# Flamingo gated block: keys and x batches 1 to 3 from host-transposed inputs, row statistics spread on chip, last keys among the first queries

## The reference

```
xn = layernorm(x);  fn = rmsnorm(ctx, fn_w)
Q = rmsnorm(xn @ Wq.T + bq, qn_w);  K = rmsnorm(fn @ Wk.T + bk, kn_w)
x = x + tanh(g_xattn) * softmax(Q K.T / sqrt(1024)) @ fn
zn = layernorm(x)
gate = softmax(zn @ W_gate.T); thr = sigmoid(zn @ W_thr + b_thr) / 8
w = max(gate - thr, 0), normalized over the 8 experts
x = x + tanh(g_ffn) * (zn @ W_base.T + b_base + 2 * sum_e w_e * (zn @ A_e.T) @ B_e.T)
```

## Time and profile before

| what | value |
|---|---|
| median of 3 runs | 527.96 us (527.92 to 528.04) |
| profiled execution | 526.89 us, span 525.1 us |
| PE busy | 500.9 us (95%) |
| DVE busy | 271.2 us (52%) |
| ACT, POOL busy | 153.0 and 153.4 us (29% each) |
| DMA, mean over the span | 83 GB/s |
| mean granted TensorE clock | 0.993 |

### The profile page before, as it was taken

One profiled execution on the slowest core, in us unless ns is written; L12 is line 12 of the kernel. 1 busy time (PEld: TensorE's weight loads), 2 busy tenths in 40 slices (PEclk: granted clock), 3 DMA queues, 4 the chain that ended last, 5 costly groups with the idle time before them and its releaser, 6 DMA issues.

```text
span 525.1 us, 7062 instructions
## 1 busy us (share of the span) xinstructions
PE 500.9 (95%) x2768; PEld 459.6 (88%) x2768; DVE 271.2 (52%) x584; ACT 153.0 (29%) x323; POOL 153.4 (29%) x123
## 2 busy tenths in 40 slices
PE   2589999999999999999988999999999999999997
PEld 2589888888888888888888999999999999999997
DVE  3887543525352532156568766456554565654423
ACT  4476444243223322354541112211112111111100
POOL 3456566312222221145273320122201222012200
PEclk9799999999999999999999999999999999999999
DMA  8643611111112001321550322113221112210012
GB/s 316 256 157 114 240 41 41 41 41 40 41 40 81 1 1 64 139 71 51 201 161 32 90 80 81 41 40 122 80 81 52 41 69 81 82 41 38 3 41 81
DMA packets 11617, 43.51 MB, mean 83 GB/s; under 512 B 1600, under 2 KB 1984, under 8 KB 11200
## 3 DMA queue, kind: packets, MB, share of 16 engines
q1 hardware_dynamic: 11584, 43.06, 22.6%
HBM read 34.67 MB, written 8.39 MB: 82 GB/s over the span
## 4 chain that ended last, share of the span: by engine, by line
PE 81%; DVE 10%; DMA 3%; POOL 2%; ACT 2%; issue 2%; SPq 0%; POOLq 0%; DVEq 0%; ACTq 0%
PE bank L399 11%; PE bank L401 11%; PE bank L400 11%; PE bank L467 10%; PE bank L468 10%; PE bank L466 10%; PE bank L332 6%; DMA bb<-b_base_dram 2%; PE bank L480 2%; DVE xn L710 2%; DVE small L697 1%; PE bank L482 1%; PE bank L481 1%; PE bank L417 1%; PE bank L416 1%
## 5 line engine op out<-in xcount | busy, mean ns | idle before, releaser
L466 PE MATMUL bank<-wch,zth 128*128 128x388 f32 x384 | 132.5, 345 | 0.0
L467 PE MATMUL bank<-wcl,zth 128*128 128x388 f32 x384 | 130.5, 340 | 0.0
L468 PE MATMUL bank<-wch,ztl 128*128 128x388 f32 x384 | 129.8, 338 | 0.0
L399 PE MATMUL bank<-xth,wqh 128*128 128x512 f32 x256 | 102.1, 399 | 0.0
L401 PE MATMUL bank<-xth,wql 128*128 128x512 f32 x256 | 100.0, 390 | 0.0
L400 PE MATMUL bank<-xtl,wqh 128*128 128x512 f32 x256 | 99.8, 390 | 0.0
L899 POOL TENSOR_TENSOR small<-small,mhalf 128x1 f32<-128x1 f32 (+1 forms) x42 | 25.8, 615 | 218.8 <-DVE small L702 190.2
L773 DVE SCALAR_TENSOR_TENSOR qtl<-bank,vecs,qth 128x512 fp32r<-128x512 f32 x32 | 24.0, 750 | 100.5 <-ACT sq L630 100.5
L466 PEld LDWEIGHTS bank<-wch,zth 128*128 128x128 f32 x384 | 72.2, 188 | 1.0
L467 PEld LDWEIGHTS bank<-wcl,zth 128*128 128x128 f32 x384 | 72.3, 188 | 0.6
L468 PEld LDWEIGHTS bank<-wch,ztl 128*128 128x128 f32 x384 | 72.1, 188 | 0.0
(11 more groups left out here) (113 smaller groups left out, 642.3 us busy)
## 6 DMA issues: line engine op xcount, KB each, us to landing
x<-x_dram SPq DMA_DIRECT2D x32, 512.0 KB, 3.3
out_dram<-x SPq DMA_DIRECT2D x15, 512.0 KB, 2.6
wc_raw<-wc_dram SPq DMA_DIRECT2D x3, 1552.0 KB, 6.1
wk_raw<-wk_dram SPq DMA_DIRECT2D x8, 512.0 KB, 10.6
wq_raw<-wq_dram SPq DMA_DIRECT2D x8, 512.0 KB, 5.5
fn_raw<-ctx_dram SPq DMA_DIRECT2D x8, 256.0 KB, 5.0
ctx_raw<-ctx_dram SPq DMA_DIRECT2D x2, 512.0 KB, 3.7
fnw<-fn_w_dram SPq DMA_DIRECT2D x1, 512.0 KB, 6.4
```

Of the source, the lines that this page charges most:

```text
L399: pe.matmul(acc[:, :], wqh[f][:, k, :], xth[b % 2][:, k, :], start=k == 0, stop=False)
L466: pe.matmul(acc, zth[z][:, k, :], wch[c][:, k, :], start=k == 0, stop=False)
L467: pe.matmul(acc, zth[z][:, k, :], wcl[c][:, k, :], start=False, stop=False)
L468: done = pe.matmul(acc, ztl[z][:, k, :], wch[c][:, k, :], start=False, stop=k == KB - 1)
```

## The change

The host now also passes two arrays: `xt`, x transposed by batch to [4, 128, 8, 512], and `ctxt`, the context transposed to [128, 8, 256].

Keys: `ct` multiplies the transposed raw context by fn_w per partition while splitting it (columns of `vecs`). The RMS root of each context row is applied after the key matmul: `rsb` transposes two columns of roots with a stride of zero, so that they lie along the free axis, and `k_out` multiplies by them. Key blocks 5 to 7 stand behind the queries 0 to 2.

Queries of batches 1 to 3: the raw transposed x is loaded; mean and root of each row are taken from a row-wise copy of x (`x_stat`), spread with two groups of stride-zero transposes (`mr`), subtracted on GpSimd (`zc`), multiplied on VectorE (`z`), and split (`z` on ScalarE, `zl` on VectorE). Batch 0 goes as before, from four buffers of its own (`xfirst`).

The diff, cut to the stage order, PE, SP and the new operations:

```diff
+        first = [("ct", 0), ("wk", 0), ("ct", 1), ("ct", 2), ("ct", 3), ("small",), ("wk", 1), ("k", 0), ("wk", 2),
+                 ("ctx_norm",), ("k", 1), ("wk", 3), ("ln_stat", 0), ("k", 2), ("rsb",), ("k_out", 0), ("ln_stat", 1),
+                 ("ln", 0), ("k_out", 1), ("wk", 4), ("ln", 1), ("k", 3), ("k_out", 2), ("xt", 0, 0), ("xt", 0, 1),
+                 ("ln_stat", 2), ("xt", 1, 0), ("xt", 1, 1), ("k", 4), ("ln_stat", 3), ("ln", 2), ("k_out", 3),
+                 ("wq", 0), ("xt", 2, 0), ("xt", 2, 1), ("ln", 3), ("k_out", 4), ("xt", 3, 0), ("xt", 3, 1), ("wk", 5),
+                 ("wq", 1)]
         for b in range(B):
             for f in range(FB):
+                if b + 1 < B and f < 2:
+                    first += [("x_stat", (b + 1) * TPB + 2 * f + j) for j in range(2)]
                 first.append(("q", b, f))
+                if b == 0 and f < 3:
+                    first += [("k", f + 5), ("k_out", f + 5)]
+                if b == 0 and f < 2:
+                    first.append(("wk", f + 6))
                 if b == 0 and f + 2 < FB:
                     first.append(("wq", f + 2))
+                if b == 0 and f == 2:
+                    first.append(("tanh",))
+                if b == 0 and f == 4:
+                    first.append(("k_norm",))
                 if f > 0:
                     first.append(("s", b, f - 1))
                 elif b > 0:
...
                 if b + 1 < B:
-                    first += [("xt", (b + 1) * TPB + u // NH, u % NH) for u in XT_AT[f]]
+                    if f == 2:
+                        first += [("mr", b + 1), ("zc", b + 1, 0)]
+                    if f >= 4:
+                        first.append(("zl", b + 1, f - 4))
+                    if 3 <= f < 7:
+                        first.append(("z", b + 1, f - 3))
+                    if 3 <= f < 6:
+                        first.append(("zc", b + 1, f - 2))
...
+        WK_DVE, WK_POOL = (2, 3), (1, 4, 5, 6, 7)
...
         def tensor(pe):
+                if stage == "rsb":
+                    acc = ring_open((stage,), "act")
+                    pe.wait_ge(g_const, CONSTS)
+                    pe.wait_ge(g_ctx, 1)
+                    transposes(acc, ctx_rs.unsqueeze(2).to_broadcast([P, 2, P]))
+                elif stage == "mr":
+                    b, = i
+                    pe.wait_ge(g_mr, b)
+                    for k in range(2):
+                        acc = ring_open((stage, b, k), "act")
+                        transposes(acc, ms[b % 2][:, k, :].unsqueeze(2).to_broadcast([P, TPB, P]))
...
                 elif stage == "q":
...
                     for k in range(KB):
+                        if b > 0 and f == 0 and k % CK == 0:
+                            pe.wait_ge(v_zl, 4 * (b - 1) + k // CK + 1)
...
         def sync(sp):
+            sp.dma_start(vecs[:, :, :], vec).then_inc(ld_vec, 16)
+            load_ct(0)
+            sp.dma_start(wk_raw[0][:, 0:4, :], wk[0][:, 0:4, :]).then_inc(ld_wk[0], 16)
+            sp.dma_start(wk_raw[0][:, 4:8, :], wk[0][:, 4:8, :]).then_inc(ld_wk0, 16)
+            load_ct(1)
+            load_ct(2)
+            load_ct(3)
+            load_wk(1)
+            load_wk(2)
+            load_ctx(0)
+            load_ctx(1)
+            load_wk(3)
+            load_x(0)
+            load_x(1)
+            load_wk(4)
+            load_x(2)
+            load_x(3)
+            load_wq(0)
+            load_wk(5)
+            load_wq(1)
+            load_wk(6)
+            load_wk(7)
+            load_x(TPB)
+            load_x(TPB + 1)
+            sp.dma_start(sc[:, 0:3], scal.to_broadcast([P, 3])).then_inc(ld_sc, 16)
+            sp.wait_ge(v_xn, 2)
+            load_wq(2)
+            sp.wait_ge(v_xn, 4)
+            load_wq(3)
+            sp.wait_ge(p_k, 2)
+            load_xt(1)
...
+                elif stage == "q" and 0 < i[0] < B - 1 and i[1] == 0:
+                    b, f = i
+                    sp.wait_ge(p_q, nq(b, 0))
+                    load_xt(b + 1)
                 elif stage == "load_fn":
                     b, = i
+                    if b == 0:
+                        sp.wait_ge(v_z, 4 * (B - 1))
+                        sp.dma_start(fnw[:, :], fn_w.to_broadcast([P, D])).then_inc(ld_fnw, 16)
...
         def scalar(act):
+                if stage == "ct":
+                    for k in range(CK * c, CK * c + CK):
+                        act.activation(cth[:, k, :], ct_raw[:, k, :], ACT.Copy, scale=fw[:, k:k + 1]).then_inc(a_cth, 1)
+                elif stage == "z":
+                    b, c = i
+                    kc = slice(CK * c, CK * c + CK)
+                    act.wait_ge(v_z, 4 * (b - 1) + c + 1)
...
+                    act.activation(xth[b % 2][:, kc, :], xt_raw[b % 2][:, kc, :], ACT.Copy).then_inc(a_zh, 1)
+                elif stage == "k_out":
+                    f, = i
+                    act.wait_ge(v_kr, f + 1)
+                    if f >= 2:
+                        act.wait_ge(g_ksum, max(1, f - 2))
+                    act.activation(ksq[f % 2][:, :], kr[f % 2][:, :], ACT.Square, bias=bk[:, f:f + 1]).then_inc(a_ksq, 1)
+                    act.wait_ge(v_kfull, f + 1)
...
                     act.activation(kt[:, f, :, 0:S], kfull[:, :].rearrange("p (b s) -> p b s", b=B),
                                    ACT.Copy).then_inc(a_kth, 1)
...
         def vector(dve):
+                elif stage == "mr":
+                    b, = i
+                    dve.wait_ge(v_xaggr, TPB * b)
+                    dve.tensor_scalar(x_tmp, ms[b % 2][:, 1, :], 1.0, LN_EPS, ALU.mult, ALU.add).then_inc(v_xvar, 1)
+                elif stage == "z":
+                    b, c = i
+                    z = xt_raw[b % 2][:, CK * c:CK * c + CK, :]
+                    dve.wait_ge(g_zc, 4 * (b - 1) + c + 1)
+                    dve.tensor_tensor(z, z, mr[:, 1:2, :].to_broadcast([P, CK, TB]), ALU.mult).then_inc(v_z, 1)
+                elif stage == "zl":
+                    b, c = i
+                    kc = slice(CK * c, CK * c + CK)
+                    dve.wait_ge(a_zh, 4 * (b - 1) + c + 1)
+                    dve.tensor_tensor(xtl[b % 2][:, kc, :], xt_raw[b % 2][:, kc, :], xth[b % 2][:, kc, :].bitcast(F32),
+                                      ALU.subtract).then_inc(v_zl, 1)
+                elif stage == "k_out":
+                    f, = i
+                    dve.wait_ge(p_k, f + 1)
...
+                    dve.tensor_tensor(kr[f % 2][:, :], acc[:, 0:S_ALL], rsb[:, :], ALU.mult).then_inc(v_kr, 1)
+                    dve.wait_ge(v_kr, f + 1)
+                    if f > 0:
+                        dve.wait_ge(v_kt, f)
+                    dve.tensor_scalar(kfull[:, :], kr[f % 2][:, :], kw[:, f:f + 1], kwb[:, f:f + 1], ALU.mult,
+                                      ALU.add).then_inc(v_kfull, 1)
                     dve.wait_ge(a_kth, f + 1)
                     dve.tensor_tensor(kt[:, f, :, S:P], kfull[:, :].rearrange("p (b s) -> p b s", b=B),
                                       kt[:, f, :, 0:S].bitcast(F32), ALU.subtract).then_inc(v_kt, 1)
...
         def gpsimd(pool):
+                elif stage == "mr":
+                    b, = i
+                    pool.wait_ge(v_xvar, b)
+                    root(ms[b % 2][:, 1, :], x_tmp, TPB).then_inc(g_mr, 1)
+                elif stage == "zc":
+                    b, c = i
+                    z = xt_raw[b % 2][:, CK * c:CK * c + CK, :]
+                    if c == 0:
+                        engine, count = ring.empty(ring.number["mr", b, 1])
+                        pool.wait_ge(ring_sem[engine], count)
+                    pool.wait_ge(ld_xt[c], 16 * b)
+                    pool.tensor_tensor(z, z, mr[:, 0:1, :].to_broadcast([P, CK, TB]), ALU.subtract).then_inc(g_zc, 1)
```

More of the change, by code:

```diff
@@ L115, in build @@
         ctx_raw = [at(f"ctx_raw{i}", [P, D], F32, r_fn + i * ROW) for i in range(2)]
+        ctx_sq = [at(f"ctx_sq{i}", [P, D], F32, r_kt + i * ROW) for i in range(2)]
         kt = at("kt", [P, FB, B, P], F32R, r_kt)
@@ L127, in build @@
         xs = [at(f"x{i}", [P, D], F32, o) for i, o in enumerate(x_at)]
+        xfirst = [at(f"xfirst{i}", [P, D], F32, r_wq + (4 + i) * ROW) for i in range(TPB)]
         xn = [at(f"xn{i}", [P, D], F32, r_xn + i * ROW) for i in range(2)]
@@ L155, in build @@
         mhalf = own("mhalf", [P, TPB])
-        vecs = own("vecs", [P, 4, FB])
+        vecs = own("vecs", [P, 5, FB])
         kw = own("kw", [P, FB])
@@ L163, in build @@
         rt = own("rt", [P, NT])
-        small = own("small", [P, 80])
+        small = own("small", [P, 120])
         gsm = [own(f"gsm{i}", [P, 40]) for i in range(2)]
@@ L919, in gpsimd @@
                     root(ln_rs(t), ln_tmp(t)).then_inc(g_rs, 1)
-                elif stage == "k" and i[0] > 0:
+                elif stage == "k_out" and i[0] > 0:
                     f, = i
```

372 lines of the change are left out of this document (205 added, 167 removed).

## The result

The changed kernel takes 560.56 us (median of 4 runs, 559.94 to 565.51) where the kernel before took 527.94 beside it: a ratio of 1.064 (95% interval 1.058 to 1.070), 32.6 us more. The direction was predicted, the size was not: 545.1 had been forecast, with 555 as the upper end. The profiled execution took 560.8 us, its span is 558.9 (525.1 before).

A forecast was written before the change was run, and what follows sets the result against it. TensorE work was taken to bound the query stage, VectorE the start. The terms -7.9 + 8.6 - 6.5 + 5.2 + 6.0 + 7.2 + 4.5 = +17.1, on 526.89 plus 1.07, gave 545.1 us, range 534 to 555.

The forecast's parts named there:

- Part 1: Query batches 1 to 3: two transpose groups instead of eight each, at 0.44 us a group, saving 7.9 us of TensorE work.
- Part 2: Keys 5 to 7 moved behind the first queries: 72 matmuls of 0.12 us, +8.6 us after the first query.
- Part 3: Start: VectorE's list of 25.1 us sets the first query, expected at 43 us (41 to 47), -6.5 us.
- So data isn't late: Start: loads ahead of x tiles 0 and 3 need 15 and 20 us, against a first query at 49.5.
- the one collision with GpSimd: Start: one VectorE clash with GpSimd allowed for in placing the first query at 43 us; no separate size stated.
- Part 4: TensorE waits for GpSimd's root ahead of the statistics transposes: +5.2 us in batch 0, +6.0 over batches 1 and 2.
- Part 5: TensorE's clock halves after idle time: 2.4 us at two places, half that at two waits, +7.2 (0 to 9.6).
- Part 6: Next batch's operand chain: GpSimd and VectorE operations may exclude each other, making operands late, +4.5 us (0 to 10).
- Rival A: Query stage: full exclusion and the clock falling at all three waits, 553 us; chance 0.17.
- B: Milder: first query at 41, no operand chain loss, clock kept over the 3.0 us waits, 536 us; chance 0.20.
- C: Start: VectorE isn't the limit, so the first query could start at 30 us, 520.4 us; chance 0.07.
- D: Query batches: root ready before TensorE comes, so no wait; 529 us, or 524.6 without operand loss; chance 0.06.

The follow-up runs named there:

- run 12: Kernel before with its own start; transposed x for batches 1 to 3, mean on VectorE, root, loads, weight splits and last operands re-placed: 522.8 us, 0.989 of the kernel before.
- run 5: Changed kernel with the outputs of keys 3 and 4 put behind the last transposed tile: 562.7 us, 1.064 of the kernel before.
- run 6: Changed kernel with the sums and roots of x tiles 2 and 3 put ahead of the outputs of keys 1 and 2: 564.1 us, 1.069 of the kernel before.
- run 7: Changed kernel with both start reorderings, late outputs of keys 3 and 4 and early sums of tiles 2 and 3: 563.0 us, 1.066 of the kernel before.
- Run 1: Changed kernel with the root of the row statistics formed ahead of query 1, transposes left in place: 548.4 us, 1.037 of the kernel before.
- run 2: Changed kernel without the subtraction of the row mean on GpSimd, so the output lacks it: 548.4 us, 1.037 of the kernel before.
- run 3: Changed kernel with 40 dummy matmuls added on TensorE ahead of the waits for the root: 556.1 us, 1.050 of the kernel before.
- run 4: Changed kernel with keys 5 to 7 and their outputs put back ahead of the first query: 580.2 us, 1.098 of the kernel before.

## Why the prediction was right and wrong

The median lies 15.5 us above the forecast and 5.6 above the range. The direction, the wait for the root and the price of the transposes and keys came as predicted; three terms of the sum were too small: the clock by 5.9 us, the operand chain by 5.5 and the start by 3.2.

**Parts 1 and 2 (transposes -7.9, keys +8.6): right.** In run 12 the part alone gave 5.7 with 1.6 idle, 7.3. A stride-zero source costs what another does: the median transpose of the statistics took 273 ns there, that of a normalized tile 272, and eight of them take 0.87 us in the chain, 0.44 a group:

```profile
68.31 0.87 PE bank L353 x8
```

**Part 3 (start -6.5): a gain, but half as large.** Two steps failed. The first is "So data isn't late", with weight 3 "landed near 14, split by 16.3". Its load landed at 15.67, the high part on ScalarE began at 15.69 and the split ended at 18.0, 1.7 later than assumed. The first 10 us moved 240 GB/s, not the 284 taken from the kernel before; that alone is 0.44 MB, or 1.1 us at 398 (an estimate). The squares of the context were hidden as predicted: ScalarE had done them at 15.55.

```profile
15.69 1.06 ACT L677 ACTIVATE wkh<-wk_raw 128x1024 fp32r<-128x1024 f32 x1
...
16.78 1.23 DVE L841 TENSOR_TENSOR wkl<-wk_raw,wkh 128x1024 fp32r<-128x1024 f32 x1 [1.03 <-ACT wkh L677]
```

The second is the one collision with GpSimd, for which the sum leaves 0.6 us (43 less 16.3, 25.1 and the wait of 1). The scaling of key 2 took 1.99 instead of 0.41, beside GpSimd's subtraction (27.25 to 29.89), and the normalization of tile 3 took 1.26 instead of 0.81, beside another (39.74 to 42.09):

```profile
27.60 0.41 DVE L908 TENSOR_TENSOR kr<-bank,rsb 128x256 f32<-128x256 f32 x1
28.05 1.99 DVE L912 TENSOR_SCALAR kfull<-kr,kw,kwb 128x256 f32<-128x256 f32 x1
...
41.38 1.26 DVE L820 TENSOR_SCALAR xn<-xfirst,small 128x1024 f32<-128x1024 f32 x1
```

That is 2.0 us of collisions, 1.4 more than allowed; with the 1.7 of the split it makes 3.1 of the 3.2 us between 43 and 46.2. The gain itself is uncertain: over the six profiles with this start the first query comes at 46.2 to 49.7, and over the four with the start of before at 49.5 to 51.5. VectorE was busy in 0.82 of the time from 20 us to the first query, not 0.85. That VectorE is the limit held only for the first part of the stretch (runs 5 to 7): its list was added up as if nothing else were between its steps. The price of 1.9 a key was right (1.8 and 2.0 for keys 0 and 1).

**Part 4 (the wait for the root, 5.2, 3.0 and 3.0): right.** Measured 5.29, 2.92 and 2.93. Run 1 shows the cause, the place in the list.

**Part 5 (clock +7.2): the mechanism right, the size not.** 13.1 was lost. The two terms of 2.4 came as 2.2 and 2.5. The two waits of 2.9 cost 1.7 and 1.6, not 1.2 each (the half of 2.4). The failed step is that it counted idle times of part 4 only: the waits of 2.6 and 2.55 made by the operand chain cost 1.7 and 3.4. The row of before that had kept the clock over 2.5 idle was one draw of several, not a rule.

**Part 6 (operand chain +4.5): half of what it was.** Measured 10.0: 1.0 and 2.6 in batch 0, 0.6 and 2.55 around the start of batch 2 and again of batch 3. The full exclusion played through had given 3.3 a batch; "I take half of 3 x 3.3, less a little" is the step that failed: measured were 3.7, 3.15 and 3.15. The doubt was wrong, but that the 10 was met so closely is in part luck. In run 2, without any subtraction on GpSimd, 2.4 of the 10.0 stayed, and batch 0, where the prediction took something off, lost the most. How much of the other 7.6 is blocking, and how much the longer chain, no run separates. The Trainium skill (SBUF — State Buffer, section "Who interferes with whom") says that a VectorE instruction with two SBUF inputs contends with a GpSimd one that reads SBUF, and calls the port pair that they share "an exclusive lock"; the trace agrees, 3.41 against 1.21 us. The prediction's term by that rule was 10. The doubt came from the start of the kernel before, played through 2 us too late with exclusion; that the fault lay elsewhere in that list is likely, but wasn't tested.

**The sum.** 16.7 us were missing: start 3.2, clock 5.9, operand chain 5.5, and 2.2 in small rests (1.5 in the query stage, 0.7 behind it); the waits for the root were 0.1 shorter than forecast. Rival A (full exclusion, clock falling at all three waits: 553) was the nearest in kind. It too left out the clock behind the chain's own waits, and the start. Rivals B, C and D didn't come.

## What to carry to other kernels

A small operation on which TensorE will wait (a root, a scale) belongs in the list ahead of the large ones of its engine, not where its result is wanted: moving it was worth 13 us from the first query on here. Before work goes to a free engine, count how long the whole chain becomes: subtraction and product took 5.3 us over GpSimd and VectorE, 3.2 on VectorE alone. And count every idle time of TensorE twice, for itself and for half-speed work that may follow it: here the clock fell behind five of six.

## What was not expected of the hardware

The clock fell behind an idle time of 2.55 us at 238.2 (0.63 over the next 9.3 us), and stayed up behind one of the same length at 179.4 in the same kernel, behind one of 2.5 in the kernel before, and in run 3 behind the one of 2.6 that had cost 1.7 us in the changed kernel. The idle time of 2.5 to 2.55 in batch 2 stands at the same place of the list in seven of these profiles: the clock fell behind it in runs 1, 3, 4 and 6, and stayed up in the changed kernel and in runs 5 and 7. So an idle time has no fixed price.

A VectorE operation with one SBUF source was blocked as well: the scaling of key 2, 1.99 instead of 0.41 us, and in run 7 a normalization of 2.62 instead of 0.80 beside a subtraction of GpSimd. In the changed kernel the sums for the statistics (0.64 to 0.70 a half row) and the low parts taken out of PSUM (0.75 for a query block, 0.68 or 0.69 for x) were as long beside GpSimd's subtractions as alone. The Trainium skill (SBUF — State Buffer, section "Who interferes with whom") names `tensor_scalar` among the operations that can take the shared port pair; these two rows, both TENSOR_SCALAR, agree.
